# Another order for the last loads, sums and stores of a two-layer block

## The chip, the core and the metric

The kernel runs on one core of a Trainium2 chip. The metric is the device time of one execution in microseconds (us). The core has TensorE (PE in the profile, its weight loads are PEld), VectorE (DVE), ScalarE (ACT), GpSimd (POOL) and SyncE (SP), and 16 DMA engines that all its queues share.

## What is computed

Two transformer layers on x of shape (4, 512, 256). The change touches only the very end of the second layer, a mixture of experts with a shared expert:

```python
topk_w, topk_idx = lax.top_k(scores, 2)
...
y = jax.nn.silu(g) * u @ w2e          # expert e
acc + cwe[:, None] * y
...
return moe + shared
...
x = x + gb * _L1_ffn_ref(h, ...)      # gb: one gate row for each of the 4 batches
```

Each token has two experts. So the last step for each token is: result of its first expert plus result of its second expert (plus, for one batch, the shared expert's output), times the gate gb of its batch, plus x.

## The kernel before

x lies in SBUF as 16 tiles of 128 tokens by 256 columns (`NT` = 16). A batch is four tiles (`TB` = 4): batch 0 is tiles 0 to 3, batch 1 tiles 4 to 7, batch 2 tiles 8 to 11, batch 3, the last, tiles 12 to 15. In float32 one tile is 128 KB.

In the last stage (`experts_stage`) 39 expert tiles run through TensorE, ScalarE and VectorE, and GpSimd sends each result to DRAM with an indirect DMA (L2973). The shared expert of batches 0 to 2 was added to x long before; that of the last batch stands behind the expert loop: hidden layer (L2454), silu and products (L2663, L2669, L2788, L2792), and down projections `down(LATE)` and `down(LATE + 1)` (L2498), whose sums stay open in PSUM banks 4 and 5 (`Y_BANK`).

When all results are in DRAM (the wait at L2437), SP reads them back. `results` has two planes, c = 0 and c = 1, the first and the second expert of each token. The work is cut into parts, slices of x's tiles:

- `PARTS` (L2373) is the order of the loads at L2440, two DMAs for each part, one for each plane: tiles 0-1, tiles 12-15 in one, tiles 2-3, tiles 4-7, tiles 8-9, tiles 10-11. That is twelve DMAs, of 256 KB for two tiles and 512 KB for four.
- `DONE` (L2376) is the order in which VectorE finishes the parts, and SP's order of stores (L2446): tiles 0-1, 2-3, 4-7, 12-13, 14-15, 8-9, 10-11.
- Parts not in `BY_TENSOR` (tiles 0-1, 2-3, 8-9) take three VectorE operations in `by_vector`: add the two planes (L2919), times the gate (L2924), add to x (L2926).
- Parts in `BY_TENSOR` (tiles 12-13, 14-15, 10-11) are summed by TensorE: a multiplication of each plane with the identity, adding in PSUM (L2638). The trace shows each of these float32 multiplications as two records, so a part is four records. VectorE then takes two operations in `by_tensor`: times the gate (L2933), add to x (L2936).
- `WITH_X`, tiles 4-7: VectorE adds the planes (L2919) and multiplies by the gate (L2922); TensorE adds that to x, which it put into PSUM banks 2 and 3 earlier (L2630), with L2646, four records; ScalarE copies the sum back to x (L2773).

TensorE's order behind `down` is: tiles 12-13, tiles 14-15, the addition for tiles 4-7 (it waits for VectorE's gate product), tiles 10-11. SP works through loads and then stores in program order: a store that waits holds all behind it.

Of the kernel before, what the change touches and what calls it, by code (L numbers as in the profile page):

```python
# [19 lines left out]
B, S = 4, 512  # L20
NT = B * S // P
TB = S // P
# [2316 lines left out]
def experts_stage(nc, t, d):  # L2339
# [10 lines left out]
    with ExitStack() as ctx:  # L2350
# [19 lines left out]
        results = wx[:, :, :, :].rearrange("p a e n -> p (a e n)")[:, 0:2 * NT * D].bitcast(F32).rearrange(  # L2370
            "p (c t n) -> p c t n", c=2, n=D)
        LAST = slice((B - 1) * TB, NT)
        PARTS = [slice(0, 2), LAST, slice(2, TB), slice(TB, 2 * TB), slice(2 * TB, 2 * TB + 2), slice(2 * TB + 2, 3 * TB)]  # L2373
        BY_TENSOR = [slice(LAST.start, LAST.start + 2), slice(LAST.start + 2, NT), PARTS[5]]
        WITH_X = PARTS[3]
        DONE = [PARTS[0], PARTS[2], PARTS[3], BY_TENSOR[0], BY_TENSOR[1], PARTS[4], PARTS[5]]  # L2376
        ADDED = [part for part in DONE if part != WITH_X]
        LATE = FS * (B - 1)
        rows_dram = t["rows_dram"].rearrange("(b p) n -> b p n", p=P)
        both = t["y_dram"][0:2 * B * S].rearrange("(c p t) n -> c p t n", c=2, t=NT)  # L2380
# [13 lines left out]
            n.sem(s) for s in ("hid_turned", "ht_high", "ht_low", "y_made", "y_scaled"))  # L2394
        results_in, pair_made = n.sems("results_in", len(PARTS)), n.sem("pair_made")
        y_sum, y_gated, x_final, stored = n.sem("y_sum"), n.sem("y_gated"), n.sem("x_final"), n.sem("stored")
        with_x_gated, x_summed, x_copied = n.sem("with_x_gated"), n.sem("x_summed"), n.sem("x_copied")

        def bank(i):
            return ps[:, i, :]  # L2400
# [17 lines left out]
        with nc.Block() as block:  # L2418

            @block.sync  # L2420
            def _(sp):
                for e in range(E):
                    sp.dma_start(wx[:, :, e, :].bitcast(F32), t["wx_dram"][e]).then_inc(wx_loaded, 16)
                sp.wait_ge(route.map_done, 2)
                sp.wait_ge(norm.turned, (B - 1) * KT)
                for c in range(2):
                    sp.wait_ge(scattered[c], B * TB * 16)
                for j in range(TILES):
                    r = j % RING1
                    if j >= RING1:  # L2430
                        sp.wait_ge(turned, j - RING1 + 1)
                        sp.wait_ge(route.addressed, j - RING1 + 1)
                    at_block = sp.value_load(route.block_i[0:1, j:j + 1], min_val=0, max_val=E * B * TB - 1)
                    sp.dma_start(rowt[:, r, :], rows_dram[bass.ds(at_block, 1)].rearrange("a p n -> (a p) n")
                                 ).then_inc(row_full[r], 16)
                for r in range(RING1):
                    sp.wait_ge(y_sent[r], len(range(r, TILES, RING1)) * 16)  # L2437
                for i, part in enumerate(PARTS):
                    for c in range(2):
                        sp.dma_start(results[:, c, part, :], both[c, :, part, :]).then_inc(results_in[i], 16)  # L2440
                for part in DONE:
                    if part == WITH_X:
                        sp.wait_ge(x_copied, 1)
                    else:
                        sp.wait_ge(x_final, ADDED.index(part) + 1)
                    sp.dma_start(t["out"][:, part, :], x[:, part, :]).then_inc(stored, 16)  # L2446
                sp.wait_ge(stored, 16 * len(DONE))

            @block.tensor
            def _(pe):  # L2450
# [21 lines left out]
                def gates(c):  # L2472
                    b, f = c // FS, c % FS
                    if b == 0:
                        pe.wait_ge(s_low, f + 1)
                    elif f == 0:
                        pe.wait_ge(norm.low_done, b)
                    if c:
                        pe.wait_ge(silu_done, c)
                    else:  # L2480
                        pe.wait_ge(route.logits_t_done, 1)
                    hidden(0, G_BANK, f, b, g_made)

                def ups(c):
                    if c:
                        pe.wait_ge(hid_done, c)
                    else:
                        pe.wait_ge(norm.mean_done, 1)
                    hidden(1, U_BANK, c % FS, c // FS, u_made)
# [109 lines left out]
                def down_of(j, e):  # L2599
                    pe.wait_ge(ht_low, j + 1)  # L2600
                    if j >= 2:
                        pe.wait_ge(y_scaled, j - 1)
                    for m, (i, (a, c)) in enumerate([(i, tc) for i in range(2) for tc in TERMS]):
                        col = KT * 2 * I + i * D
                        last = nc.tensor.matmul(ps[:, 6 + j % 2, 0:D], turned_hidden(j, a)[:, i, :],  # L2605
                                                wx[0:IH, c, bass.ds(e, 1), col:col + D].rearrange("p e n -> p (e n)"),
                                                start=(m == 0), stop=(m == 5))
                    last.then_inc(y_made, 1)

                pe.wait_ge(upd_done, B - 1)  # L2610
                pe.wait_ge(rows_read, 2 * B)
                pe.wait_ge(hid_done, LATE)
                at_expert = {}
                for s in range(TILES + 3):
# [7 lines left out]
                    if s >= 3:  # L2622
                        down_of(s - 3, at_expert.pop(s - 3))
                gates(LATE)
                ups(LATE)
                gates(LATE + 1)
                ups(LATE + 1)
                pe.wait_ge(t_hid, TILES)
                for i in range(2):
                    nc.tensor.matmul(bank(X_BANK + i), t["ident"][:, :],  # L2630
                                     x[:, WITH_X.start + 2 * i:WITH_X.start + 2 * i + 2, :].rearrange("p t n -> p (t n)"),
                                     start=True, stop=False)
                down(LATE)
                down(LATE + 1)
                for i, part in enumerate(BY_TENSOR):
                    pe.wait_ge(results_in[1 if i < 2 else 5], 32)
                    for c in range(2):
                        last = nc.tensor.matmul(bank(Y_BANK + i), t["ident"][:, :],  # L2638
                                                results[:, c, part, :].rearrange("p t n -> p (t n)"),
                                                start=(i == 2 and c == 0), stop=(c == 1))  # L2640
                    last.then_inc(pair_made, 1)
                    if i == 1:
                        pe.wait_ge(with_x_gated, 1)
                        for half in range(2):
                            tt = WITH_X.start + 2 * half
                            last = nc.tensor.matmul(bank(X_BANK + half), t["ident"][:, :],  # L2646
                                                    results[:, 0, tt:tt + 2, :].rearrange("p t n -> p (t n)"),
                                                    start=False, stop=True)
                        last.then_inc(x_summed, 1)

            @block.scalar
            def _(act):
# [76 lines left out]
                for s in range(TILES + 3):  # L2729
# [25 lines left out]
                    if j >= 0:  # L2755
# [5 lines left out]
                        elif j == 0:  # L2761
# [10 lines left out]
                act.wait_ge(x_summed, 1)  # L2772
                nc.scalar.copy(x[:, WITH_X, :].rearrange("p (i t) n -> p i (t n)", i=2), ps[:, X_BANK:X_BANK + 2, :]  # L2773
                               ).then_inc(x_copied, 1)

            @block.vector
            def _(dve):
# [131 lines left out]
                def gate_rows(part):  # L2909

                    b = part.start // TB
                    return t["gate"][:, 3, b:b + 1, :].to_broadcast([P, part.stop - part.start, D])

                def by_vector(part):

                    i, n = PARTS.index(part), DONE.index(part)
                    y = results[:, 0, part, :]
                    dve.wait_ge(results_in[i], 32)
                    nc.vector.tensor_tensor(y, y, results[:, 1, part, :], ALU.add).then_inc(y_sum, 1)  # L2919
                    dve.wait_ge(y_sum, sum(p not in BY_TENSOR for p in DONE[:n + 1]))  # L2920
                    if part == WITH_X:
                        nc.vector.tensor_tensor(y, y, gate_rows(part), ALU.mult).then_inc(with_x_gated, 1)  # L2922
                        return
                    nc.vector.tensor_tensor(y, y, gate_rows(part), ALU.mult).then_inc(y_gated, 1)  # L2924
                    dve.wait_ge(y_gated, ADDED.index(part) + 1)
                    nc.vector.tensor_tensor(x[:, part, :], x[:, part, :], y, ALU.add).then_inc(x_final, 1)  # L2926

                def by_tensor(part):

                    i, n = BY_TENSOR.index(part), ADDED.index(part)  # L2930
                    y = results[:, 0, part, :]
# [5 lines left out]

                for part in DONE:
                    if part in BY_TENSOR:
                        by_tensor(part)  # L2940
# [176 lines left out]
```

## Time and profile before

| | us |
|---|---|
| median of 3 runs | 1146.12 |
| lowest and highest | 1146.06, 1146.46 |
| the profiled execution, as timed | 1145.18 |
| its span from first to last instruction | 1143.5 |
| last result landed in DRAM, reads begin | 1119.8 into the span |
| VectorE's last instruction ends | 1140.6 into the span |

Positions below are us from the start of the span. A group of rows is from one view; in the timeline a row is a run of like instructions, with the start, the length from first start to last end, and in brackets the engine's idle time before it and what ended it. Of a DMA the view of issues gives the size and the time from issue to landing. PEclk in the views by stretch is the granted share of TensorE's full clock of 2.4 GHz; 0.50 is the other level, 1.2 GHz.

### The profile page before, as it was taken

The page shows a single profiled execution, that of the slowest core. Times are in us where ns is not written, and L with a number is a line of the kernel's source. Part 1 is how long each engine was busy: PE and PEld are TensorE (multiplying, and loading weights), DVE is VectorE, ACT ScalarE, POOL GpSimd, SP SyncE. Part 2 cuts the span into 40 slices and gives each one's busy share as a digit, 9 for nine tenths or more (in the row PEclk, how much of TensorE's full clock was granted, in tenths as well). Part 3 has the DMA queues.
Part 4 walks back from the last instruction along what each step waited for, and adds up shares of the span by engine and source line. Part 5 has one row for each costly group of instructions (what it writes and reads, how often), then busy time and mean ns, then how long its engine had stood idle before and what let it go on. Part 6 is the DMA issues. An engine that isn't in the chain of part 4 may idle for free. (4 is left out here: it accounts for less than half of the span.)

```text
span 1143.5 us, 22333 instructions
## 1 busy us (share of the span) xinstructions
PE 1060.2 (93%) x7536; PEld 923.7 (81%) x7536; DVE 895.2 (78%) x1817; ACT 736.2 (64%) x1399; POOL 334.6 (29%) x335
## 2 busy tenths in 40 slices
PE   5888888879999999999999999999999997979996
PEld 4656666658899899899898898898998986769994
DVE  5788988857788788788788788788788787867775
ACT  4679797767766666666666666666666654625661
POOL 3353544442311201211111111111111234753440
PEclk9889999979999999999999999999999998989999
DMA  7210001010401311311311211221221291824436
GB/s 256 94 52 16 16 6 44 14 50 23 137 21 50 112 47 47 108 45 52 100 51 53 94 58 53 89 62 53 80 71 54 83 45 66 355 98 116 123 98 234
DMA packets 67881, 92.13 MB, mean 81 GB/s; under 512 B 22658, under 2 KB 46338, under 8 KB 66787
## 3 DMA queue, kind: packets, MB, share of 16 engines
q1 hardware_dynamic: 64402, 81.83, 24.6%
q0 software_dynamic: 3408, 9.39, 2.2%
q8 instruction: 41, 0.67, 0.2%
q14 instruction: 30, 0.24, 0.1%
HBM read 46.35 MB, written 42.75 MB: 78 GB/s over the span
## 5 line engine op out<-in xcount | busy, mean ns | idle before, releaser
L1551 PE MATMUL all_psum<-all_h_parts,attn_wp 128*128 128x512 f32 x1140 | 297.6, 396 | 0.0
L1551 PEld LDWEIGHTS all_psum<-all_h_parts,attn_wp 128*128 128x128 f32 x1140 | 209.8, 189 | 39.7
L1723 ACT CAST attn_pp<-attn_p 128x512 fp32r<-128x512 f32 (+3 forms) x256 | 117.4, 459 | 187.8 <-DVE attn_p L1831 185.7
L1812 DVE TENSOR_TENSOR attn_pp<-attn_p,attn_pp 128x512 fp32r<-128x512 f32 (+3 forms) x256 | 198.0, 773 | 6.5 <-ACT attn_pp L1723 6.5
L1970 POOL TENSOR_TENSOR all_gate<-all_gate,attn_sq 128x512 f32<-128x512 f32 x64 | 84.7, 1324 | 369.8 <-ACT attn_sq L1734 369.7
L1630 PE MATMUL all_psum<-attn_qkp 128*128 128x512 f32 (+3 forms) x768 | 164.9, 323 | 3.7 <-DVE attn_qkp L1812 3.7
L1577 PE MATMUL all_psum<-attn_pp,attn_vp 128*128 128x512 f32 (+3 forms) x768 | 163.8, 322 | 1.0 <-DVE attn_pp L1812 0.5
L1577 PEld LDWEIGHTS all_psum<-attn_pp,attn_vp 128*128 128x128 f32 x768 | 129.4, 189 | 21.6 <-issue 1.2
L1630 PEld LDWEIGHTS all_psum<-attn_qkp 128*128 128x128 f32 x768 | 124.8, 190 | 12.6 <-issue 4.3
L1831 DVE TENSOR_TENSOR attn_p<-all_psum,attn_mask 128x512 f32<-128x512 f32 (+3 forms) x256 | 123.5, 482 | 2.1 <-PE all_psum L1630 0.9
L1054 DVE TENSOR_REDUCE front_top<-all_psum 128x2 f32<-128x256 f32 (+3 forms) x128 | 99.4, 815 | 17.8 <-PE all_psum L695 16.8
L1812 DVE TENSOR_TENSOR attn_yp<-attn_y,attn_yp 128x512 fp32r<-128x512 f32 x64 | 45.6, 712 | 77.2 <-ACT attn_yp L1731 77.2
L853 ACT ACTIVATE front_probs<-all_psum 128x1024 f16<-128x1024 f32 (+3 forms) x128 | 83.5, 705 | 30.3 <-PE all_psum L704 30.1
L1546 PE MATMUL all_psum<-attn_wp,all_h_parts 128*128 128x256 f32 x768 | 100.7, 280 | 0.0
L1561 PE MATMUL all_psum<-all_wop,attn_yp 128*128 128x256 f32 x744 | 96.5, 278 | 0.6 <-DVE attn_yp L1812 0.6
L1812 DVE TENSOR_TENSOR attn_qkp<-attn_qk,attn_qkp 128x512 fp32r<-128x512 f32 x128 | 88.3, 690 | 10.7 <-ACT attn_qkp L1698 10.7
L1546 PEld LDWEIGHTS all_psum<-attn_wp,all_h_parts 128*128 128x128 f32 x768 | 94.6, 188 | 0.1
L1561 PEld LDWEIGHTS all_psum<-all_wop,attn_yp 128*128 128x128 f32 x744 | 91.0, 188 | 0.8 <-DVE attn_yp L1812 0.8
L1698 ACT CAST attn_qkp<-attn_qk 128x512 fp32r<-128x512 f32 x128 | 79.5, 621 | 4.1
L1695 ACT ACTIVATE attn_qk<-all_psum 128x512 f32<-128x512 f32 x128 | 75.8, 592 | 0.3 <-PE all_psum L1551 0.3
L1812 DVE TENSOR_TENSOR attn_vp<-attn_v,attn_vp 128x512 fp32r<-128x512 f32 x64 | 44.3, 692 | 31.7 <-ACT attn_vp L1716 31.7
L702 PE MATMUL all_psum<-front_qt,front_kt 128*128 128x512 f16 (+3 forms) x256 | 59.5, 306 | 9.3 <-ACT front_probs L853 6.1
(381 smaller groups left out, 1899.5 us busy)
## 6 DMA issues: line engine op xcount, KB each, us to landing
expert_rows<-attn_empty SPq DMA_DIRECT2D x8, 2080.0 KB, 12.7
expert_weight_parts<-all_wraw SPq DMA_DIRECT2D x32, 304.0 KB, 2.4
experts_wx<-expert_weight_parts SPq DMA_DIRECT2D x8, 1216.0 KB, 16.6
all_wraw<-in_w1p SPq DMA_DIRECT2D x8, 1024.0 KB, 5.9
all_yacc<-expert_rows SPq DMA_DIRECT2D x39, 130.5 KB
all_wraw<-in_wx SPq DMA_DIRECT2D x16, 304.0 KB, 3.0
attn_mask<-decay_masks SPq DMA_DIRECT2D x16, 256.0 KB, 2.6
all_x<-in_x SPq DMA_DIRECT2D x4, 512.0 KB, 7.0
```

Of the source, the lines that this page charges most:

```text
L853: nc.scalar.activation(prob(gg, pr, j), halves(ev)[:, :, 0:S - j * P], ACT.Exp, scale=D0 ** -0.5).then_inc(exp_done, 1)
L1054: nc.vector.tensor_reduce(top[:, tt, h:h + 2], halves(ev)[:, :, 0:(tt + 1) * P], AX.X, ALU.max).then_inc(top_done, 1)
L1546: last = nc.tensor.matmul(out[:, i * 2 * P:(i + 1) * 2 * P], hh[:, a, k, tt * P:(tt + 1) * P], wp[:, c, k, col:col + 2 * P], start=(m == 0 ...
L1551: last = nc.tensor.matmul(out, wp[:, a, k, col:col + P], hh[:, c, k, b * S:(b + 1) * S], start=(m == 0), stop=(m == 5))
L1561: last = nc.tensor.matmul(ps[:, Y_BANK + i, half * D:(half + 1) * D], yp[:, a, h, tt * P:(tt + 1) * P], wop[:, c, h, :], start=(m == 0), s ...
L1577: last = nc.tensor.matmul(ps[:, O_BANK + h, j * P:S], vp[:, b % 2, a, j, h * P:(h + 1) * P], pp[:, h, c, OFF[j]:OFF[j] + S - j * P], start ...
L1630: last = nc.tensor.matmul(bank(task)[:, 0:S - j * P], qkp[:, h, a, 1, j * P:(j + 1) * P], qkp[:, h, c, 0, j * P:S], start=(m3 == 0), stop= ...
L1698: nc.scalar.copy(qkp[:, (unit + 1) % 2, 0, which, :], qk[:, which, :]).then_inc(hi_sem, 1)
L1723: nc.scalar.copy(pp[:, u % 2, 0, cols], p[:, cols]).then_inc(p_hi, 1)
L1812: nc.vector.tensor_tensor(out, whole, high.bitcast(F32), ALU.subtract).then_inc(ready, 1)
L1831: nc.vector.tensor_tensor(p[:, cols], bank(task)[:, 0:S - j * P], mask[:, u % 2, 0:S - j * P], ALU.mult).then_inc(p_masked, 1)
L1970: nc.gpsimd.tensor_tensor(cols, cols, sq[:, h, :], ALU.add).then_inc(summed, 1)
```

## The change

The loads come in the order 0-1, 2-3, 4-7, 12-13, 14-15, 8-9, 10-11, so that the load of tiles 12-15 is now two parts and there are fourteen DMAs; this is also VectorE's order, which is as before. Tiles 8-9 go from `by_vector` to `by_tensor`: TensorE sums them too, between the addition for tiles 4-7 and the sum of tiles 10-11. Each part summed by TensorE has a PSUM bank of its own (4 to 7). In the stores tiles 12-13 go ahead of tiles 4-7.

```diff
-        PARTS = [slice(0, 2), LAST, slice(2, TB), slice(TB, 2 * TB), slice(2 * TB, 2 * TB + 2), slice(2 * TB + 2, 3 * TB)]
-        BY_TENSOR = [slice(LAST.start, LAST.start + 2), slice(LAST.start + 2, NT), PARTS[5]]
-        WITH_X = PARTS[3]
-        DONE = [PARTS[0], PARTS[2], PARTS[3], BY_TENSOR[0], BY_TENSOR[1], PARTS[4], PARTS[5]]
+        LAST = [slice((B - 1) * TB, (B - 1) * TB + 2), slice((B - 1) * TB + 2, NT)]
+        PARTS = [slice(0, 2), slice(2, TB), slice(TB, 2 * TB), LAST[0], LAST[1], slice(2 * TB, 2 * TB + 2),
+                 slice(2 * TB + 2, 3 * TB)]
+        BY_TENSOR = LAST + PARTS[5:]
+        WITH_X = PARTS[2]
+        DONE = PARTS
         ADDED = [part for part in DONE if part != WITH_X]
+        STORED = ADDED[:3] + [WITH_X] + ADDED[3:]
...
-                for part in DONE:
+                for part in STORED:
...
-                    pe.wait_ge(results_in[1 if i < 2 else 5], 32)
+                    pe.wait_ge(results_in[PARTS.index(part)], 32)
...
-                                                start=(i == 2 and c == 0), stop=(c == 1))
+                                                start=(i >= 2 and c == 0), stop=(c == 1))
```

## Rows read from the trace of the kernel before

**Rows 1.** The page's first part: busy us, share of span, instructions.
```profile
PE 1060.2 (93%) x7536; PEld 923.7 (81%) x7536; DVE 895.2 (78%) x1817; ACT 736.2 (64%) x1399; POOL 334.6 (29%) x335
```
**Rows 2.** The chain that ended last, its end: start, length, what.
```profile
1123.29 8.78 DMA experts_wx<-expert_results
...
1132.10 1.24 DVE experts_wx L2919
1133.36 1.22 DVE experts_wx L2922
...
1139.93 0.69 DVE all_x L2936
```
**Rows 3.** Loads issued at 1120.2, 1121.15, 1122.1, 1122.55, 1123.25, 1126.25: size, us to landing.
```profile
experts_wx<-expert_results SPq DMA_DIRECT2D x1, 256.0 KB, 3.4
experts_wx<-expert_results SPq DMA_DIRECT2D x1, 512.0 KB, 6.6
experts_wx<-expert_results SPq DMA_DIRECT2D x1, 256.0 KB, 6.9
experts_wx<-expert_results SPq DMA_DIRECT2D x1, 512.0 KB, 7.6
experts_wx<-expert_results SPq DMA_DIRECT2D x1, 512.0 KB, 8.8
experts_wx<-expert_results SPq DMA_DIRECT2D x1, 256.0 KB, 8.7
```
**Rows 4.** Stores issued at 1126.75 and 1140.65, the first and the last: the same.
```profile
out<-all_x SPq DMA_DIRECT2D x1, 256.0 KB, 7.7
out<-all_x SPq DMA_DIRECT2D x1, 256.0 KB, 2.4
```
**Rows 5.** Timeline of the end: TensorE.
```profile
1125.82 0.28 PE L2498 MATMUL all_psum<-experts_w_second,experts_hidp 128*128 128x256 f32 x1
1127.75 3.70 PE L2638 MATMUL all_psum<-experts_wx,all_ident 128*128 128x512 f32 x8 [1.66 <-DMA experts_wx<-expert_results]
1134.64 1.98 PE L2646 MATMUL all_psum<-experts_wx,all_ident 128*128 128x512 f32 x4 [3.19 <-DVE experts_wx L2922]
1136.46 1.88 PE L2638 MATMUL all_psum<-experts_wx,all_ident 128*128 128x512 f32 x4
```
**Rows 6.** Timeline of the end: VectorE and ScalarE.
```profile
1125.10 0.69 DVE L2926 TENSOR_TENSOR all_x<-all_x,experts_wx 128x512 f32<-128x512 f32 x1
1136.66 1.01 ACT L2773 COPY all_x<-all_psum 128x1024 f32<-128x1024 f32 x1 [13.75 <-PE all_psum L2646]
1139.21 0.68 DVE L2933 TENSOR_TENSOR experts_wx<-all_psum,all_gate 128x512 f32<-128x512 f32 x1
```
**Rows 7.** Line L2440, SP's issues: duration ns min/median/max, first and last start.
```profile
L2440 SPq DMA_DIRECT2D experts_wx<-expert_results x12: 331/436/794, 1119.8 to 1126.3; - x12
```
**Rows 8.** By stretch: length, busy us of PE, PEld, DVE, ACT, POOL; PEclk, DMA.
```profile
237.10:241.49 4.39, 0.00 (x1) 0.03 (x1) 1.91 (x3) 1.55 (x3) 0.04 (x2) 0.69 0.00 0
955.55:958.97 3.42, 3.42 (x18) 3.42 (x18) 2.74 (x4) 1.12 (x2) 1.28 (x1) 0.50 0.00 0
963.05:966.28 3.23, 0.00 (x1) 0.00 (x1) 1.46 (x13) 0.83 (x3) 0.84 (x7) 0.92 0.00 0
1023.45:1026.19 2.74, 0.00 (x1) 0.03 (x1) 2.45 (x2) 0.00 (x0) 0.00 (x0) 0.93 0.19 52
1027.23:1034.06 6.83, 6.10 (x22) 5.52 (x23) 2.59 (x12) 1.96 (x6) 0.00 (x0) 0.50 0.43 117
1131.45:1134.64 3.19, 0.00 (x2) 0.00 (x1) 2.51 (x3) 0.00 (x0) 0.00 (x0) 1.00 0.95 360
```
**Rows 9.** TensorE's timeline: twelve L2454 records at full clock, six at 0.50.
```profile
1115.76 2.97 PE L2454 MATMUL all_psum<-all_h_parts,experts_w_first 128*128 128x512 f32 x12
...
972.81 2.87 PE L2454 MATMUL all_psum<-all_h_parts,experts_w_first 128*128 128x512 f32 x6
```
**Rows 10.** Stores of the result, all seven.
```profile
DMA to landing us min/median/max: 2.4/3.0/7.7
```

## The prediction

> **What bounds the kernel now.** TensorE is busy for 93% of the span [rows 1], but that says little here: the change touches only what happens after the last expert result is in DRAM, the last 24 of 1143.5 us. So I read the chain that ended last, from there on [rows 2]. There SP issues loads from 1119.8 on. From 1123.29, when the eighth load (the second one of tiles 4-7) is issued, it runs through that load for 8.78 us. At 1132.10 it reaches VectorE, and it stays on VectorE without a gap until 1139.93 + 0.69 = 1140.62. What follows is the last store: issued at 1140.65, landed 2.4 us later [rows 4], and the span ends at 1143.5. So two things set the end: when tiles 4-7 land, and 8.5 us of VectorE behind them. The rest of the span and what lies around it (1145.18 - 1143.5 = 1.7 us) stay.
>
> When does a load land? Issue time plus time to landing [rows 3] gives 1123.6 for the first part (2 tile pairs of 256 KB, counting both planes: "units"), 1127.75 for tiles 12-15 (6 units in), 1129.0 for tiles 2-3 (8 units), 1130.15 for the first half of tiles 4-7 (10 units), 1132.1 for the second half (12 units) and 1135.0 for the last load (16 units). From 8 to 12 units that is 0.77 us for a unit. The first store, issued behind all loads, took 7.7 us where the last took 2.4 [rows 4]: what is issued later stands behind the loads, so the stores' new times do not hold up the loads.
>
> TensorE in this stretch [rows 5] ends its shared-expert work at 1126.1, waits for tiles 12-15 until 1127.75, sums them (8 records, 3.70 us), and pauses 3.19 us for VectorE's gate product. Four records after a pause take 1.98 us; the next four add 3.70 - 1.98 = 1.72 us. That gives the price of one part summed by TensorE.
>
> **The order of loads.** Tiles 2-3 now land at 4 units instead of 8. The third load of before, its first 512 KB, would be those 4 units; interpolating from 2 units at 1123.6 to 6 at 1127.75 gives 1125.7, and VectorE is busy with tiles 0-1 until 1125.8 [rows 6]. Its three operations on tiles 2-3, 0.69 us each like the one in [rows 6] and with about 0.03 between them, then run from about 1125.9 to 1128.0. Tiles 4-7 land at 8 units, sixth issue, as tiles 2-3 did: 1129.0, 3.1 us earlier. Their two operations, 2.48 us [rows 2], end at 1131.5. Tiles 12-13 land at 10 units, 1130.15 to 1130.5; I take 1130.3. Tiles 14-15 at 12 units: 1132.1. Tiles 8-9 at 14 and 10-11 at 16 units: about 1133.6 and 1135.0. The change issues two loads more. At 0.33 to 0.79 us each [rows 7] they lie behind the eighth issue, and the last load may land up to 0.8 us later than 1135.0, which nobody waits for (below). SP's first store is issued about 1 us later and lands behind the loads anyway.
>
> **Tiles 8-9 move to TensorE.** VectorE loses one operation of 0.69 us (two are left of its three). TensorE gains four records, 1.72 us. Before, TensorE had pauses to spare; with tiles 12-13 landing last of what it needs first, it has not. Its chain is now: tiles 12-13, 14-15, the addition for 4-7, tiles 8-9, tiles 10-11, twenty records in a row. Start 1130.3; tiles 12-13 ready 1132.3 (+1.98); tiles 14-15 landed at 1132.1 when TensorE is free at 1132.0, ready 1134.1; addition for 4-7 ready 1135.8 (its gate product has been there since 1131.5); tiles 8-9 ready 1137.5; tiles 10-11 ready 1139.25. VectorE takes each in 1.41 us (1139.21 to 1140.62 [rows 2, 6]), less than TensorE's 1.72, so it waits for TensorE each time and ends at 1139.25 + 1.41 = 1140.7. Before it ended at 1140.62. **At full clock the sum is +0.1 us: the 3.1 us won at the landing of tiles 4-7 go to the wait for TensorE.** The bounds: tiles 12-15 landing 0.6 us earlier (at the 0.63 us for a unit that the trace shows from 6 to 8 units), or tiles 12-13 at 1132.1, where the eighth issue landed before, 1.8 later.
>
> **TensorE's clock.** TensorE used to pause from 1126.1 to 1127.75; now it pauses until 1130.3, for 4.2 us. What did pauses do to the clock? The trace of before has pauses of 4.39, 3.23 and 2.74 us in [rows 8], without one matmul in them: the granted clock is 0.69 of full over the first and 0.92 over the second, so it fell inside them. Over the third it is 0.93 and reads so because of the end of an earlier fall; 0.50 stands right behind it (1027.23 to 1034.06). Only the 3.19 us pause of the tail, 1131.45 to 1134.64, shows 1.00. So I expect that the new 4.2 us pause costs the clock. At 0.50, six records of L2454 took 2.87 us, at full clock twelve took 2.97 [rows 9]: work takes twice the time. The two stretches at 0.50 [rows 8] lasted 3.4 and 6.8 us with TensorE busy in nearly all of both, so the loss is 1.7 to 3.4 us, less the part that is over before TensorE starts again. I take 4.4 us of work at 1.2 GHz, a loss of 2.2 us, and all of it is on the path, since TensorE's chain sets the end. The Trainium skill ("TensorE: Matmul & The Clock Gate", the table under "Why this matters for your kernels") says that a pause between bursts of matmuls drops the clock back to half and advises against it; by its rule the sum is the same +2.3, and this case's trace agrees in three of the four pauses named here, but not in the 3.19 us one.
>
> **Stores.** The seven stores follow one another in SP's order, the last one landing 2.4 us after issue [rows 4]. ScalarE's copy of tiles 4-7 starts at 1136.66 [rows 6]; at full clock it would start at 1135.8, at the lower one at about 1138.0. Tiles 12-13, ready at 1133.7 or 1135, no longer stand behind it: 256 KB leave the queue early. That keeps the last store from being held; its 2.4 us from issue to landing is already the shortest of the seven, whose median is 3.0 [rows 10]. A further gain I bound by the spread of these two, 0.6 us, a loss by the same, and take nothing.
>
> **The sum.** 1145.18 + 0.1 + 2.2 = 1147.5 us. The median of before is 0.94 above its profiled execution. That may be the very same thing: if the 3.19 us pause drops the clock in the timed runs, the eight records behind it (3.70 us) take up to 3.4 us longer, of which VectorE, which needs the last sum at 1139.21 and gets it at 1138.34, feels up to 2.5 us, and 0.8 us for a low stretch of 3.4 us. I therefore forecast from 1145.18, not from the median.
>
> **The rivals.**
> 1. The clock stays at full, as after the 3.19 us pause. Then 1145.18 + 0.1 = 1145.3, with the landing's -0.6 and the store's -0.6 down to 1144.1, and 0.9 up if the median's distance is no matter of clock: 1146.2. For it: one pause of the tail did no harm. Against: the longer ones all did. 19%.
> 2. The other side: slower by over 0.2%. Loads land by their place in the queue and not by bytes, so tiles 12-13 come at 1132.1, with the eighth issue. TensorE's chain starts 1.8 us later, everything behind it too, and the pause is 6 us. With the clock's 2.2: 1145.18 + 1.8 + 0.1 + 2.2 = 1149.3. It decides once the landing is later than 1130.3 + (1148.4 - 1147.5) = 1131.2. For it: SP's issues differ in length, from 0.33 to 0.79 us [rows 7], and are not paced by bytes. Against: the loads of different size land evenly by bytes. 10%.
> 3. VectorE's order wins what it seems to: TensorE's sums are not the bound, because records of two planes overlap more than seen. Then the last load (1135.0) + 1.98 + 1.41 = 1138.4 sets the end, 2.2 us earlier: 1143.0. Against: the last four of eight records in a row took 0.43 us each [rows 5]. 4%.
> 4. The change does nothing to the order that counts (an earlier load is hidden anyway). That is the full-clock case with its +0.1 and has its price.
>
> The forecast, with a clock loss of 1.2 to 3.4 us, holds 67% and spans 1146.5 to 1149.4.
>
> **How the numbers follow.** 0.2% of 1146.12 is 2.3 us, about what a measurement of this kernel can tell from no change: 1143.8 to 1148.4 is "same". Slower: a fifth of the forecast's case (clock loss over 3.1 us, or the median's 0.9 on top) 13%, most of rival 2, 8%: 21%. Faster: 4%. Same: 75%. For 8 in 10 the range leaves out rival 3, the lower part of rival 1 and the top of rival 2: 1144.9 to 1149.4.
>
> **What would show it.** After: the loads of tiles 4-7 landing near 1129 on the same scale; TensorE starting L2638 near 1130.3 with 4 us of idle before it; L2638 and L2646 in one unbroken row to the end; VectorE waiting for PE before each L2933; PEclk at 0.50 somewhere in 1129 to 1136. It is wrong if VectorE has no waits behind 1131, if TensorE's row has pauses, or if twenty records at full clock take other than 8.9 us.

## The result, and the profile after

| | before | after |
|---|---|---|
| median of 20 runs, us | 1146.26 | 1148.06 |
| lowest and highest | 1144.03, 1148.60 | 1146.11, 1151.11 |
| the profiled execution, its span | 1145.18, 1143.5 | 1149.82, 1148.1 |
| first read-back issued, into the span | 1119.83 | 1121.19 |
| VectorE's end behind that issue | 20.8 | 24.5 |
| tail: from that issue to the end of the span | 23.6 | 26.9 |

The ratio is 1.0018, 95% interval 1.0011 to 1.0024: the changed kernel is slower by 1.3 to 2.8 us, the forecast said 1147.5. The stages ahead of the last one differ by some us from one execution to the next, so I compare profiles by the **tail**, measured from SP's first read-back issue; landings are given from there too ("behind the first issue").

The chain that ended last, after the change (start, length, what), against [rows 2]:

```profile
1121.19 0.33 SPq L2443
...
1124.42 8.64 DMA experts_wx<-expert_results
...
1133.10 5.95 PE all_psum L2641 x8
1139.06 1.72 PE all_psum L2649 x4
1140.77 3.45 PE all_psum L2641 x8
...
1144.24 0.70 DVE experts_wx L2936
...
1144.97 0.69 DVE all_x L2939
```

The load at its head is another one: the eighth issue is now the second plane of tiles 12-13. Behind it VectorE has gone from the chain but for its last two operations; 11.1 us of TensorE stand in its place, twenty records in a row.

The timeline shows the pause ahead of them and VectorE waiting for each sum ([rows 5] and [rows 6] answer to it):

```profile
1133.10 5.95 PE L2641 MATMUL all_psum<-experts_wx,all_ident 128*128 128x512 f32 x8 [5.63 <-DMA experts_wx<-expert_results]
1136.92 0.69 DVE L2936 TENSOR_TENSOR experts_wx<-all_psum,all_gate 128x512 f32<-128x512 f32 x1 [2.90 <-PE all_psum L2641]
1138.89 1.88 PE L2649 MATMUL all_psum<-experts_wx,all_ident 128*128 128x512 f32 x4
1139.09 0.69 DVE L2936 TENSOR_TENSOR experts_wx<-all_psum,all_gate 128x512 f32<-128x512 f32 x1 [0.76 <-PE all_psum L2641]
1140.61 3.60 PE L2641 MATMUL all_psum<-experts_wx,all_ident 128*128 128x512 f32 x8
1142.53 0.69 DVE L2936 TENSOR_TENSOR experts_wx<-all_psum,all_gate 128x512 f32<-128x512 f32 x1 [2.02 <-PE all_psum L2641]
1144.24 0.69 DVE L2936 TENSOR_TENSOR experts_wx<-all_psum,all_gate 128x512 f32<-128x512 f32 x1 [0.30 <-PE all_psum L2641]
```

By stretch, with the columns of [rows 8]: the pause, TensorE's work at the lower level of its clock (0.50, which is 1.2 GHz), and the rest:

```profile
1127.48:1133.10 5.62, 0.00 (x0) 0.00 (x0) 3.61 (x5) 0.00 (x0) 0.00 (x0) 0.80 1.01 372
1133.10:1137.67 4.57, 4.57 (x6) 1.97 (x7) 1.63 (x3) 0.00 (x0) 0.00 (x0) 0.50 0.72 273
1137.67:1144.20 6.53, 6.53 (x16) 2.60 (x14) 3.43 (x5) 1.01 (x1) 0.00 (x0) 1.00 0.34 134
```

The clock fell inside the pause, and the first six of the eight records ran wholly or in part at half speed: 5.95 us for what took 3.70 before [rows 5], a loss of 2.25 us.

Five loads and the last store, as in [rows 3] and [rows 4] (issued at 1122.53, 1123.47, 1123.95, 1124.42, 1128.72; the store at 1145.69):

```profile
experts_wx<-expert_results SPq DMA_DIRECT2D x1, 256.0 KB, 6.5
experts_wx<-expert_results SPq DMA_DIRECT2D x1, 512.0 KB, 8.0
experts_wx<-expert_results SPq DMA_DIRECT2D x1, 256.0 KB, 6.6
experts_wx<-expert_results SPq DMA_DIRECT2D x1, 256.0 KB, 8.6
experts_wx<-expert_results SPq DMA_DIRECT2D x1, 256.0 KB, 8.3
...
out<-all_x SPq DMA_DIRECT2D x1, 256.0 KB, 2.0
```

Issue plus landing time, less 1121.19: tiles 2-3 complete at 7.8, tiles 4-7 at 10.3, tiles 12-13 at 11.9. These are the times of the second load of each part. Both loads of a part count up one semaphore, by 16 each (`then_inc(results_in[i], 16)`, and the readers wait for 32), and the view gives the first sixteen arrivals to the first issue and the other sixteen to the second. So the second load's time is when the part was complete; the first load's only says when half of the arrivals were in (for tiles 12-13 at 9.4, 1123.95 + 6.6), and not which plane they belonged to. The trace has the time of each arrival, and in them one sees what "complete" waits for:

| arrivals, us behind the first issue | first | half of them | last but one | last |
|---|---|---|---|---|
| tiles 2-3, changed | 3.8 | 4.3 | 7.2 | 7.8 |
| tiles 12-13, changed | 8.5 | 9.4 | 11.1 | 11.9 |

Most of tiles 2-3 was there early (28 of the 32 arrivals by 5.5), but the last two came at 7.2 and 7.8.

### The profile page after: what moved, and what is told of

It reads as the page before. It is cut to its first block and busy times, and to the rows that moved or that the text cites. A ratio compares the mean times of both kernels' runs of the same rounds, so it can differ in the third digit from the quotient of the medians.

```text
span 1148.1 us, 22342 instructions
## 1 busy us (share of the span) xinstructions
PE 1067.0 (93%) x7540; PEld 927.0 (81%) x7540; DVE 894.4 (78%) x1816; ACT 736.1 (64%) x1399; POOL 335.2 (29%) x335
## 3 DMA queue, kind: packets, MB, share of 16 engines
q1 hardware_dynamic: 64690, 81.83, 24.5%
## 5 line engine op out<-in xcount | busy, mean ns | idle before, releaser
L1577 PEld LDWEIGHTS all_psum<-attn_pp,attn_vp 128*128 128x128 f32 x768 | 128.9, 189 | 21.6 <-issue 1.5
L1812 DVE TENSOR_TENSOR attn_qkp<-attn_qk,attn_qkp 128x512 fp32r<-128x512 f32 x128 | 88.1, 688 | 10.7 <-ACT attn_qkp L1698 10.7
L702 PE MATMUL all_psum<-front_qt,front_kt 128*128 128x512 f16 (+3 forms) x256 | 62.1, 316 | 8.3 <-ACT front_probs L853 6.1
```

Source lines behind the costliest of these rows:

```text
L1577: last = nc.tensor.matmul(ps[:, O_BANK + h, j * P:S], vp[:, b % 2, a, j, h * P:(h + 1) * P], pp[:, h, c, OFF[j]:OFF[j] + S - j * P], start ...
L1812: nc.vector.tensor_tensor(out, whole, high.bitcast(F32), ALU.subtract).then_inc(ready, 1)
```

## The experiments

The theory: the tail of the changed kernel is the landing of tiles 12-13, then TensorE's twenty records, part of them at half clock because of the pause in front, then 1.4 us of VectorE and the store. The rivals: the order of stores costs something; VectorE is as tight as TensorE; the clock is a detail beside the late landing; the fall of the clock was an accident of one execution. The kernels with a ratio were timed against the kernel before on their own chip. A tail is that of one profiled execution; where a kernel was profiled twice the two tails differ by 0.1 us.

| kernel | tail, us | ratio to before | 95% interval |
|---|---|---|---|
| before | 23.64 | | |
| before again | 23.55 | | |
| changed | 26.90 | 1.0018 | 1.0011 to 1.0024 |
| changed again | 26.99 | | |
| changed, no pause | 24.47 | 0.9999 | 0.9990 to 1.0007 |
| changed, tiles 8-9 by VectorE | 25.77 | 1.0019 | 1.0010 to 1.0028 |
| changed, loads of before | 23.90 | 1.0015 | 1.0004 to 1.0026 |
| changed, stores in the old order | 26.69 | 1.0016 | 1.0007 to 1.0026 |
| before, no pause | 23.27 | 1.0003 | 0.9992 to 1.0013 |
| changed, planes together | 23.93 | 1.0004 | 0.9993 to 1.0016 |
| changed, planes swapped | 26.18 | | |
| changed, planes together, no pause | 22.57 | 0.9992 | 0.9980 to 1.0004 |
| early sums | 22.35 | 0.9986 | 0.9974 to 0.9999 |
| early sums, planes together | 21.68 | 0.9983 | 0.9974 to 0.9991 |

**The pause and the clock.**

```diff
                 down(LATE + 1)
+                for m in range(22):
+                    nc.tensor.matmul(bank(G_BANK), wsh(0, 0)[:, 0:P], hh[:, 0, 0, (B - 1) * S:B * S],
+                                     start=(m == 0), stop=(m == 21))
                 for i, part in enumerate(BY_TENSOR):
```

> The changed kernel with 22 extra matmuls (128x512, into a PSUM bank that is no longer read, about 5.2 us) between the shared expert's down projection and the wait for tiles 12-13, so that TensorE doesn't pause there. Measured by the tail: from SP's first read-back issue to the end of the span, 23.6 us before the change, 26.9 after it. Theory (TensorE's chain of twenty records from the landing of tiles 12-13 on, at half clock for part of it): granted clock 1.00 throughout the tail, the first eight records take 3.7 us instead of 5.95, tail 24.6. Rival (the late landing alone or the stores set the end, the clock is idle detail): tail stays at 26.9. If the extra matmuls disturb the loads, tiles 12-13 land later than 11.9 us behind the first issue.

Timeline of TensorE in that kernel:

```profile
1125.97 5.29 PE L2639 MATMUL all_psum<-all_h_parts,experts_w_first 128*128 128x512 f32 x22
1131.58 3.70 PE L2643 MATMUL all_psum<-experts_wx,all_ident 128*128 128x512 f32 x8 [0.32 <-DMA experts_wx<-expert_results]
1135.12 1.88 PE L2651 MATMUL all_psum<-experts_wx,all_ident 128*128 128x512 f32 x4
```

3.70 us, as at full clock before, and a tail of 24.47 where 24.6 was expected. The loads landed as before (tiles 12-13 at 11.7). Work that computes nothing takes 2.4 us off the tail, 2.25 of them TensorE's eight records, so the clock was on the path. The timed runs agree: no difference from before is left, and the interval lies below that of the changed kernel.

**Tiles 8-9 by VectorE again.**

```diff
-        BY_TENSOR = LAST + PARTS[5:]
+        BY_TENSOR = LAST + PARTS[6:]
```

> The changed kernel with tiles 8-9 summed by VectorE again; orders of loads and stores as in the changed kernel. Theory (TensorE's chain sets the end): the chain has 16 records, its last four come 1.7 us earlier, VectorE does its three operations in its wait: tail 25.2 (from 26.9). Rival (VectorE is as tight as TensorE, so that the 0.69 us more there cost): tail 26.9 or up to 27.6.

VectorE ended 22.79 us behind the first issue, 1.68 earlier than in the changed kernel (24.47): the four records are on the path, as the theory has it. But its last two operations follow the one before without a wait:

```profile
1138.98 1.88 PE L2641 MATMUL all_psum<-experts_wx,all_ident 128*128 128x512 f32 x4
...
1140.25 0.69 DVE L2929 TENSOR_TENSOR all_x<-all_x,experts_wx 128x512 f32<-128x512 f32 x1
1140.90 0.69 DVE L2936 TENSOR_TENSOR experts_wx<-all_psum,all_gate 128x512 f32<-128x512 f32 x1
```

TensorE is done at 1140.86 and VectorE free at 1140.94, so the two are level. The four stores now stand close together at the end, and the last took 2.54 us from issue to landing instead of 2.00. That gave back 0.54, and the tail is 25.77, not 25.2. In the timed runs this gain doesn't show (1.0019 against 1.0018); by them alone the experiment would decide nothing.

**The loads of before.** `LOADS` lists tiles 0-1, 12-15 in one, 2-3, 4-7, 8-9, 10-11.

```diff
-                for i, part in enumerate(PARTS):
+                for part, whose in LOADS:
                     for c in range(2):
-                        sp.dma_start(results[:, c, part, :], both[c, :, part, :]).then_inc(results_in[i], 16)
+                        sp.dma_start(results[:, c, part, :], both[c, :, part, :]).then_inc(results_in[whose[0]], 16)
...
-                    pe.wait_ge(results_in[PARTS.index(part)], 32)
+                    pe.wait_ge(results_in[3 if i < 2 else PARTS.index(part)], 32)
```

> The changed kernel with the loads in the order and sizes of before (tiles 0-1, 12-15 in one, 2-3, 4-7, 8-9, 10-11); tiles 8-9 by TensorE and the new order of stores stay. Theory: TensorE starts at 7.9 us behind the first issue instead of 11.9, the clock stays up at first, but the addition for tiles 4-7 waits for VectorE's product at 14.8 as before, and tiles 8-9 and 10-11 queue behind it: 14.8 + 1.98 + 1.72 + 1.72 = 20.2, VectorE ends at 21.6 instead of 20.8 before: tail 24.4 where the pause of 3.2 us leaves the clock alone, up to 26.5 where it doesn't. Rival (the order of loads costs nothing, the sum on TensorE and the stores are the loss): tail 26.9.

The tail is 23.90, 0.5 below the 24.4 expected, most of it because the last store took 2.01 us and not 2.4. In the profile 3.0 us of the 3.3 lost come with the order and the sizes of the loads, by the start of TensorE (11.9 behind the first issue, 8.2 here) and by the clock, which stayed at 1.00 here. TensorE still had a pause of 2.69 us. The timed runs don't bear this out: the ratio, 1.0015, is higher than a tail 0.3 us longer would give, and its interval holds the changed kernel's 1.0018; that other executions lose clock behind that pause, with twelve records and no slack after it, would fit, but no run shows it.

**The stores.**

```diff
-        STORED = ADDED[:3] + [WITH_X] + ADDED[3:]
+        STORED = DONE
```

> The changed kernel with the stores in VectorE's order again (tiles 4-7 ahead of 12-13). Theory (stores have slack): tail within 0.4 us of 26.9, the last store lands 2.0 to 2.4 us after its issue. Rival (the order of stores matters to the end): the last store is held behind the others and lands 2.7 us or more after its issue, tail 27.6.

Tail 26.69, the last store 2.01 us from issue to landing; tiles 12-13 were complete 0.3 us earlier in this execution, as much as the 0.2 by which the tail is shorter. Stores have slack, and their order is worth nothing here.

**Does the pause always cost, and does the kernel before pay too?**

> The changed kernel itself, profiled once more. Theory (a pause of 5.6 us always costs the clock): granted clock 0.50 over part of TensorE's first twelve records, the first eight take 5 to 7.4 us instead of 3.70, tail 26 to 27.7. Rival (the fall was an accident of one execution): 1.00 throughout, tail 24.6.

The first eight records took 5.77 us behind a pause of 5.91, tail 26.99. All five profiles with fourteen loads and TensorE idle until tiles 12-13 landed (pauses of 4.8 to 5.9 us) show the fall.

> The kernel before itself, profiled once more, to see what its 3.2 us pause does to the clock in another execution. Theory: a pause of the tail may be followed by a fall or not; if it is, the addition for tiles 4-7 and the sum of tiles 10-11 take up to twice their 3.70 us, VectorE waits for the last sum, and the tail (from SP's first read-back issue to the end) is 24.4 to 26.2 us instead of 23.6. Rival (this pause never costs the clock): granted clock 1.00 until TensorE is done, tail 23.4 to 23.8.

In this execution the clock fell behind the shorter pause, the one ahead of tiles 12-15. It was still at 1.00 for the first 1.43 us of TensorE's row and at 0.50 for the next 3.42:

```profile
1134.55 5.40 PE L2638 MATMUL all_psum<-experts_wx,all_ident 128*128 128x512 f32 x8 [2.04 <-DMA experts_wx<-expert_results]
...
1142.78 1.88 PE L2638 MATMUL all_psum<-experts_wx,all_ident 128*128 128x512 f32 x4
```

5.40 us instead of 3.70, and yet a tail of 23.55: the sums were ready before VectorE wanted them (TensorE's row ended 13.7 us behind the first issue, and VectorE took its first sum at 14.6). A fall that costs TensorE 1.7 us is free before the change; one of 2.25 us is paid in full after it. The case that I had expected, a fall behind the 3.2 us pause, didn't come up.

> The kernel before with extra matmuls in both its pauses (6 ahead of the wait for tiles 12-15, 12 ahead of the wait for VectorE's gate product). Theory (the kernel before pays for its 3.2 us pause in some executions): tail 23.6 us in the profile, and the timed runs faster than those of before by up to 0.1%. Rival (before pays nothing): ratio 1.000, tail 23.6.

The edit is the same loop, of 6 and of 12 matmuls. Tail 23.27, 0.4 shorter than in the first profile, and tiles 4-7 were complete 0.4 earlier too in this execution. Ratio 1.0003 with 0.1% either way: no sign that the kernel before pays for its pauses, nor proof that it never does.

**What sets the landing.**

```diff
-                    for c in range(2):
-                        sp.dma_start(results[:, c, part, :], both[c, :, part, :]).then_inc(results_in[i], 16)
+                    sp.dma_start(results[:, :, part, :].rearrange("p c t n -> p c (t n)"),
+                                 both[:, :, part, :].rearrange("c p t n -> p c (t n)")).then_inc(results_in[i], 16)
```

> The changed kernel with one load for both planes of a part, seven loads of 512 KB and 1 MB instead of fourteen. It asks what sets the landing of tiles 12-13, 11.8 us behind the first issue where the bytes ahead of them suggested 10.4. By place in the queue (each issue costs 0.43 us and more): tiles 12-13, now the fourth issue, land at 10 us or earlier and the tail falls by up to 1.5 us from 26.9. By bytes: landing at 10.4 either way. If the second plane's data are slow for a reason of their own, landing stays at 11.8 and the tail at 26.9.

The load of tiles 12-13, issued at 1126.51, 1.45 behind the first:

```profile
experts_wx<-expert_results SPq DMA_DIRECT2D x1, 512.0 KB, 8.3
```

It landed at 9.73, 2.1 us earlier than in the changed kernel, though the same bytes stood ahead of it. So bytes alone didn't hold tiles 12-13 back; splitting each part into two loads did. The arrivals at their counter say more:

| arrivals of tiles 12-13, us behind the first issue | first | half of them | last but one | last |
|---|---|---|---|---|
| changed | 8.5 | 9.4 | 11.1 | 11.9 |
| changed again | 8.7 | 9.7 | 11.5 | 12.1 |
| changed, planes together | 8.5 | 8.8 | 9.1 | 9.7 |
| changed, planes swapped | 8.5 | 9.6 | 10.7 | 11.0 |

The first arrival comes at the same 8.5 us; with two loads to a part the arrivals are spread over 3.4 us, with one load over 1.2. One thing this edit doesn't separate: the part's only load is also issued 1.8 us earlier than the second of the two was (1.45 against 3.23), and from its issue it took nearly as long (8.3 us against 8.6). TensorE's pause shrank to 3.50 us and its loss to 1.4 (eight records in 5.11), tail 23.93. The timed ratio fell to 1.0004.

> The changed kernel with the second plane of each part issued ahead of the first. In the changed kernel the loads of the second plane take 8.0 to 8.6 us to land where those of the first, issued between them, take 6.1 to 7.2. Theory (an effect of the place in the pair, or of the one issued behind the other): again the second issue of each pair is the late one, tiles 12-13 complete at 11.8, tail 26.9. Rival (the second plane's region in DRAM is the slow one): now the first issue of each pair takes about 8 us, the second 6 to 7, and tiles 12-13 are complete up to 0.5 us earlier.

Tiles 12-13 were complete at 10.99, where the five profiles with the planes in the first order had 11.6 to 12.1, and the tail is 0.7 shorter. That is more than the 0.5 us the rival allowed, but it is one execution. The times of the two issues (9.60 and 10.99) can't decide between the two answers: both planes count up one semaphore, and the view would give the later half of the arrivals to the second issue whichever plane was late. A counter for each plane would tell; no run has one. Why the arrivals of a part in two loads spread so far stays open.

**Both causes away.** The kernel with planes together and 14 extra matmuls in the pause:

> The changed kernel with one load for both planes of a part and 14 extra matmuls (about 3.4 us) in TensorE's pause. Both causes are taken away: the late landing of tiles 12-13 and the clock. Theory: landing at 9.7, clock 1.00, twenty records in 8.9 us, VectorE ends at 20.0, tail 22.4 (before 23.6), timed 0.05 to 0.15% faster than before. Rival (a further cause, VectorE or stores): tail 23.6 or more.

```profile
1130.84 3.70 PE L2643 MATMUL all_psum<-experts_wx,all_ident 128*128 128x512 f32 x8 [0.27 <-DMA experts_wx<-expert_results]
```

Landing at 9.77, full clock, VectorE's end at 20.12, tail 22.57. With both causes away the whole loss of 3.3 us is gone, and 1.1 us more. In the timed runs this version is faster than the changed kernel (the intervals don't overlap); against the kernel before, the ratio points the same way, but its interval holds 1.

**A version that beats both.** It keeps the loads of before and gives tiles 8-9 to TensorE, but sums them and tiles 10-11 ahead of the addition for tiles 4-7, on which only ScalarE's copy waits:

```diff
-        DONE = [PARTS[0], PARTS[2], PARTS[3], BY_TENSOR[0], BY_TENSOR[1], PARTS[4], PARTS[5]]
+        DONE = [PARTS[0], PARTS[2], BY_TENSOR[0], PARTS[3], BY_TENSOR[1], PARTS[4], PARTS[5]]
...
                     last.then_inc(pair_made, 1)
                     if i == 1:
+                        for m in range(8):
+                            nc.tensor.matmul(bank(G_BANK), wsh(0, 0)[:, 0:P], hh[:, 0, 0, (B - 1) * S:B * S],
+                                             start=(m == 0), stop=(m == 7))
+                    if i == 3:
                         pe.wait_ge(with_x_gated, 1)
```

VectorE finishes tiles 12-13 ahead of tiles 4-7. ScalarE's copy and the store of tiles 4-7 are in two halves, the second of them the last store of all, and 6 more extra matmuls stand ahead of the wait for tiles 12-15. The second version has one load for both planes of a part besides.

> A version put together from the findings: loads as before the change; tiles 8-9 summed by TensorE, but the sums of tiles 8-9 and 10-11 ahead of the addition for tiles 4-7; VectorE finishes tiles 12-13 ahead of tiles 4-7; ScalarE copies and SP stores tiles 4-7 in two halves; extra matmuls in TensorE's pauses (6 and 8). Theory (bounds are TensorE's chain from a landing on and its clock): clock 1.00 throughout, VectorE ends 19.4 us behind the first issue instead of 20.8, the last store is the second half of tiles 4-7, tail 22.6 (before 23.6, changed kernel 26.9); timed 0.1 to 0.2% faster than before. Rival (stores bound the end): tail 23.3 or more, no difference in time from before.

> The version with early sums (e8), with one load for both planes of a part. There the chain ran from the landing of tiles 8-9 (13.3 us behind the first issue) through twelve records of TensorE, ScalarE's copies and the last store, tail 22.35 us. Theory (landings come earlier with fewer issues, tiles 8-9 at 12.6 as in e7): tail 21.6, timed 0.15 to 0.25% faster than before. Rival (VectorE, which ended 18.9 us behind the first issue, is as tight): tail 22.3.

Tails of 22.35 and 21.68, where 22.6 and 21.6 were expected. The second one's timeline:

```profile
1127.29 3.60 PE L2641 MATMUL all_psum<-experts_wx,all_ident 128*128 128x512 f32 x8
1130.32 2.42 PE L2647 MATMUL all_psum<-all_h_parts,experts_w_first 128*128 128x512 f32 x8
1132.59 3.60 PE L2641 MATMUL all_psum<-experts_wx,all_ident 128*128 128x512 f32 x8
1136.02 1.88 PE L2652 MATMUL all_psum<-experts_wx,all_ident 128*128 128x512 f32 x4
...
1137.94 0.58 ACT L2781 COPY all_x<-all_psum 128x512 f32<-128x512 f32 x1 [0.27 <-PE all_psum L2652]
```

TensorE starts 7.5 us behind the first issue and has no pause worth the name. With a ratio of 0.9983 (0.9974 to 0.9991) this version is 1.0 to 3.0 us faster than the kernel before, and its tail is 5.2 us shorter than the changed kernel's. How much each of its edits gives was not measured.

## Why the prediction was right, and where it wasn't

- **What bounds before**, and that TensorE would take over: right. VectorE waits for TensorE ahead of each of its last four parts, and the twenty records are one unbroken row.
- **The price of the sums**: 8.9 us for twenty records at full clock. Measured 1133.10 to 1144.2, 11.1 us, less the 2.25 lost to the clock: 8.9; and 8.85 straight out in both kernels with the pause filled.
- **The clock**: 2.2 us forecast, 2.25 measured, and shown to be on the path by the kernel without the pause. The size was in part luck: the profiles of the changed kernel and its variants with that pause show eight records in 5.77 to 6.11 us, a loss of 2.1 to 2.4; with the shorter pause of the planes together it was 1.4. The rule of the Trainium skill ("TensorE: Matmul & The Clock Gate", "Why this matters for your kernels"), that a pause between bursts of matmuls brings the clock down, holds for all pauses of 4.8 us and more here; it doesn't tell the 2.04 us pause with a fall behind it from the 3.19 us one without.
- **The landings** were mis-sized. The step "tiles 2-3 now land at 4 units" gave 5.9 us behind the first issue and measured 7.8; tiles 4-7 came at 10.3 instead of 9.2; tiles 12-13 at 11.9 instead of 10.5. I read an even pace of bytes out of [rows 3], and the row for 10 units was not what I took it for: 1130.15, "the first half of tiles 4-7", is the time when half of the arrivals of both planes were in, and no part was complete then. A part is complete with its last arrival, and the last ones came late: in the kernel before the fourth load completed its part at 7.9, and so it did in the changed kernel, with a third fewer bytes up to it. Completed parts alone, 8 and 12 units, give 10.75 behind the first issue for 10 units; the other 1.1 us are not in those rows. Rival 2 had this mechanism, landing by the place in the queue, with 10%; its point of decision, 1131.2, is 11.4 behind the first issue, and tiles 12-13 came later than that. So the case that came is the forecast's clock with most of rival 2's delay, 1.4 of its 1.8 us.
- **The stores**: nothing forecast. Their order is worth nothing, but the last store took 2.0 us instead of 2.4. The last four no longer stand close together; with tiles 8-9 by VectorE they did again, and it took 2.54. That is inside the bound of 0.6, and it hid part of the landing's 1.4.
- **The sum**: a tail of 23.6 + 2.3 = 25.9 forecast, 26.9 measured, from 1.4 more and 0.4 less. By the profiled executions the distance is 4.6 us, of which 1.4 lie ahead of the tail, where nothing was changed. By the medians of twenty runs it is 1.8, and 1148.06 is 0.6 above the forecast. That nearness is luck in part: the forecast started from an execution 1.1 us below the median, and put the tail's growth at 2.3 us where the profiles have 3.3.
- **That the median of before stands above its profiled execution because of the clock in the tail**: not borne out. Without the pauses the kernel before is no faster (1.0003), and the spread of runs, 1144.0 to 1148.6, is far wider than the 0.4 us between the three profiled tails of that kernel, with its pauses and without. Forecasting from 1145.18 left out that the profiled execution was in the lower third of that spread.
- **Open**: the timed runs put the loss at 1.3 to 2.8 us, two profiles of each kernel at 3.3 to 3.4. For the kernel with no pause the ratio is lower than its tail, for the one with the loads of before it is higher.

## What to carry to other kernels

Work moved to an engine with idle time is free only if the idle time lies behind the input that it waits for: here the new order put TensorE's first input last but three, and made one long pause in front out of two shorter ones, one in front and one inside. Before reordering loads, read when each part was complete, by its last arrival, and not a mean pace of bytes; where two loads share a semaphore the profile can't time them one by one. When an engine must wait for a transfer and then sets the end, look at what the wait does to its clock; a stretch of useless matmuls gave back 2.4 us here, and the loads landed as before.

## What the runs showed of the hardware

- A part of 512 KB loaded as two DMAs of 256 KB had its first arrival at 8.5 us behind the first issue and its last at 11.9; as one DMA of 512 KB it had them at 8.5 and 9.7, with the same bytes ahead of it (tiles 12-13, changed kernel and planes together).
- SP's issue of a load of one plane took 0.33 us for the first, 0.42 to 0.44 for the next four, and from the sixth on anything from 0.43 to 1.25 us, while the DMA engines were busy for about 80% of the time or more.
- The granted clock fell to 0.50 behind a pause of 2.04 us in one execution of the kernel before, and didn't fall behind one of 3.19 us in another, nor behind one of 2.69 us with the loads of before. It fell in or behind every pause of 3.50 us (planes together) and more, 4.8 to 5.9 us in five profiles. So below 3.5 us the length of the pause alone didn't decide in this stage.
